# A two-layer graph network on one core: the second layer's tiles in a new order, half of x1 kept on chip

## What is computed

```python
h = jnp.maximum(_layernorm(x), 0.0)
x = x + elu(graph_attention(h, adj) @ W_out + b_out)      # 16 heads, masked softmax
h = jnp.maximum(_layernorm(x), 0.0)
# second layer: q, k, v = h @ W.T + b
z = scale * (q @ k.T) * adj
z = jnp.where(z == 0.0, -10000.0, z)
out = x + relu(softmax(z, axis=1) @ v)
```

## Time and profile before

| | us |
|---|---|
| median of 3 runs | 469.98 (469.42 to 470.12) |
| the profiled execution | 469.46 |
| its span, first to last instruction | 467.5 |
| busy in the span: TensorE, VectorE | 395.3, 369.1 |
| busy: GpSimd, ScalarE | 257.9, 246.1 |

### The profile page before, as it was taken

How to read it: one execution, slowest core, us unless ns; L and a number is a source line. 1 busy time by engine, 2 the same in 40 slices (tenths; PEclk the granted TensorE clock), 3 DMA queues, 4 the chain that set the end, 5 groups by cost and what they waited for, 6 DMA issues and landing times.

```text
span 467.5 us, 6241 instructions
## 1 busy us (share of the span) xinstructions
PE 395.3 (85%) x2058; PEld 282.6 (60%) x2070; DVE 369.1 (79%) x731; ACT 246.1 (53%) x511; POOL 257.9 (55%) x268
## 2 busy tenths in 40 slices
PE   7999999997899998989959879789891998866960
PEld 3888887784777887865737546456581565423430
DVE  4999999987899999977999996898445789957300
ACT  4389777766899998924424433444432433312310
POOL 2335241242788677766757648835337787871330
PEclk9599999999899999999989998899996899995995
DMA  8989998510000123445535527632136678873451
GB/s 315 399 320 332 390 339 299 201 70 2 6 6 5 23 72 92 104 126 182 188 87 166 162 91 205 197 122 91 46 113 192 199 174 168 165 162 43 52 65 19
DMA packets 26997, 70.02 MB, mean 150 GB/s; under 512 B 7893, under 2 KB 8149, under 8 KB 24789
## 3 DMA queue, kind: packets, MB, share of 16 engines
q0 software_dynamic: 13056, 38.45, 31.5%
q1 hardware_dynamic: 13904, 31.16, 18.3%
q10 hardware_dynamic: 4, 0.00, 0.0%
HBM read 52.47 MB, written 17.13 MB: 149 GB/s over the span
## 4 chain that ended last, share of the span: by engine, by line
POOL 31%; PE 15%; issue 15%; DVE 9%; DMA 1%; ACT 1%; DVEq 0%; POOLq 0%
PE psum L1303 8%; POOL s_shared L1231 7%; PE psum L1401 5%; POOL s_shared L1254 4%; POOL out_dram L1243 4%; POOL s_x L1254 4%; POOL s_shared L1212 3%; POOL s_rs L1242 3%; POOL out_dram L1259 3%; DVE s_shared L796 2%; DVE s_shared L794 2%; POOL s_x L1249 2%; DVE s_x L810 1%; DMA w_out<-h_dram,s_near_rank 1%; POOL w_out L1254 1%
## 5 line engine op out<-in xcount | busy, mean ns | idle before, releaser
L1064 ACT ACTIVATE s_shared<-psum,seq_all 128x320 bf16<-128x320 f32 x192 | 81.7, 568 | 6.1 <-PE psum L1303 4.4
L1303 PE MATMUL psum<-s_shared 128*128 128x198 bf16 x768 | 75.2, 254 | 9.6 <-POOL s_shared L1212 9.6
L1303 PEld LDWEIGHTS psum<-s_shared 128*128 128x128 bf16 x768 | 67.9, 98 | 17.4 <-POOL s_shared L1212 9.9
L555 PE MATMUL psum<-w_seq,hT 128*128 128x272 f32 x256 | 63.8, 405 | 0.4 <-ACT w_seq L416 0.4
L1325 PE MATMUL psum<-w_out,hT 128*128 128x512 f32 x128 | 60.7, 619 | 0.4
L555 PEld LDWEIGHTS psum<-w_seq,hT 128*128 128x128 f32 x256 | 49.4, 197 | 10.3 <-ACT w_seq L416 0.5
L1347 PE MATMUL psum<-w_qk,s_early 128*128 128x257 f32 x240 | 54.5, 379 | 0.0
L1347 PEld LDWEIGHTS psum<-w_qk,s_early 128*128 128x128 f32 x240 | 44.4, 190 | 6.0
L1231 POOL DMA_INDIRECT s_shared<-seq_dram,tab x30 | 37.7, 1255 | 11.3 <-issue 8.9
L1325 PEld LDWEIGHTS psum<-w_out,hT 128*128 128x128 f32 x128 | 26.0, 203 | 25.8 <-issue 24.9
L1212 POOL TENSOR_TENSOR s_shared<-s_shared 128x1056 f32<-128x1056 f32 x16 | 31.1, 1945 | 15.2 <-DVE s_shared L796 15.2
(11 more groups left out here) (264 smaller groups left out, 756.8 us busy)
## 6 DMA issues: line engine op xcount, KB each, us to landing
adj_ring<-in_adj_dram SPq DMA_DIRECT2D x16, 1024.0 KB, 8.1
seq_dram<-seq_all POOLq DMA_DIRECT2D x16, 264.0 KB, 4.7
x_ring<-in_x_dram SPq DMA_DIRECT2D x16, 256.0 KB, 8.4
h_dram<-h_t SPq DMA_DIRECT2D x16, 256.0 KB, 2.4
w_seq<-in_L_gnn_W_seq_dram SPq DMA_DIRECT2D x1, 1024.0 KB, 5.7
w_q<-in_L_gnn_W_q_dram SPq DMA_DIRECT2D x1, 1024.0 KB, 13.7
w_k<-in_L_gnn_W_k_dram SPq DMA_DIRECT2D x1, 1024.0 KB, 15.9
w_v<-in_L_gnn_W_v_dram SPq DMA_DIRECT2D x1, 1024.0 KB, 9.0
```

The source lines that it names most:

```text
L555: last = pe.matmul(bank[2 + 2 * (t % 2) + i][:, 0:SX // 2], hT[:, t % 2, c * P:(c + 1) * P], w_seq[:, c, i * (SX // 2):(i + 1) * (SX // 2) ...
L1064: last = act.activation(ind[i][:, j, PAD:], bank[4 + i][:, 0:LN], ACT.Sign, bias=seq_all[:, j, D + n:D + n + 1])
L1303: last = pe.matmul(acc(i)[:, k, 0:3 * W2], ind[i][:, j, k * P:(k + 1) * P], rhs.rearrange("p t w -> p (t w)"), start=(j == 0 and k != 1), ...
```

## The change

In the second layer the tiles come in the order `SEQ1`: the tile without slots first, then rising numbers of slots. The gathers of all 40 slots come ahead of all outputs. They go to other places (`row`): the last ones over the first ones again, and no longer into x1. So tiles of x1 can stay on chip: the first layer scatters only the first eight (`STORED`), for which ScalarE's relu and an accumulating output are kept; for the other eight VectorE adds x1 to the relu of the product (`add_x`) and a plain scatter writes the sum. VectorE's order is written out by hand. TensorE transposes the last h1 tile ahead of query 12, does queries 12 to 14 behind the column sums and 15 behind the transposes of the first tile; the products of the first tile still come ahead of the second tile's transposes. Some of the first layer's gathers are issued one step earlier.

```diff
-GATHER = {0: ((5, 5, 8),), 1: ((7, 0, 3),), 2: ((7, 3, 5),), 3: ((9, 0, 3),), 4: ((9, 3, 4), (11, 0, 2)),
-          5: ((11, 2, 3), (12, 0, 2)), 6: ((14, 0, 2),), 7: ((13, 0, 3),), 8: ((15, 0, 3),)}
+GATHER = {0: ((5, 6, 8), (7, 0, 2)), 1: ((7, 2, 5),), 2: ((9, 0, 3),), 3: ((9, 3, 4), (11, 0, 2)), 4: ((11, 2, 3),),
+          5: ((12, 0, 2),), 6: ((14, 0, 2),), 7: ((13, 0, 3),), 8: ((15, 0, 3),)}
...
-U1_AT = {4: 14, 6: 15}
...
+SEQ1 = [4, 0, 1, 2, 3, 6, 8, 10, 12, 14, 11, 13, 15, 9, 7, 5]
+POS1 = {t: p for p, t in enumerate(SEQ1)}
+ROW1 = {t: sum(SLOTS[i] for i in SEQ1[:p]) for p, t in enumerate(SEQ1)}
+EXP1_AT = {2: 1, 4: 2, 8: 3, 11: 4}
+BASES_AT = {0: (1, 2, 3), 1: (4,), 3: (5, 6, 7), 5: (8, 9), 9: (10, 11, 12), 10: (13,), 12: (14, 15)}
+WEIGHTS_AT = {0: 1, 3: 2, 5: 3, 9: 4, 12: 5}
+STORED = 8
+BY_ACT = [p for p in range(T) if TURN[SEQ1[p]] < STORED]
+BY_DVE = [p for p in range(T) if TURN[SEQ1[p]] >= STORED]
...
         def u_bank(t):
-            return 6 if t >= EARLY or U_NO[t] % 2 else 4
+            return 6 if U_NO[t] % 2 else 4
...
-        o_t = [lone[:, 0, :], lone[:, 1, :], lone[:, 2, :], bv_bc[:, :]]
-        PARTS = [(0, 4), (5, 2), (7, 2), (9, 3), (12, 4)]
-        first_of = {t0: g for g, (t0, n) in enumerate(PARTS)}
-        with_slots = [sum(n > 0 for n in SLOTS[:k]) for k in range(T + 1)]
+        PARTS = [slice(0, 4), slice(6, 11, 2), slice(12, T, 2), slice(9, T, 2), slice(5, 8, 2)]
+        PART_TILES = [len(range(T)[part]) for part in PARTS]
+        FIRSTS = (1,)
+        with_slots = [sum(SLOTS[t] > 0 for t in SEQ1[:p]) for p in range(T + 1)]
...
-        def row(k):
+        ROWS_EARLY = FLAT_ROWS + C + LONE + 1
+        ROWS_AGAIN = ROWS_EARLY + EARLY - 4
+
+        def row(t, s):
+            k = ROW1[t] + s
+            if k >= ROWS_AGAIN:
+                k -= ROWS_AGAIN
             if k < FLAT_ROWS:
                 return shared[:, k * D:(k + 1) * D]
-            if k < FLAT_ROWS + T:
-                return x1[:, k - FLAT_ROWS, :]
-            return w_out[:, k - FLAT_ROWS - T, :]
+            if k < FLAT_ROWS + C:
+                return w_out[:, k - FLAT_ROWS, :]
+            if k < FLAT_ROWS + C + LONE:
+                return lone[:, k - FLAT_ROWS - C, :]
+            if k < ROWS_EARLY:
+                return bv_bc[:, :]
+            return early[:, 4 + k - ROWS_EARLY, 0:D]
...
                 def scores1(g):
...
-                    for t in range(t0, t0 + n):
-                        dot(t)
-                    if t0 == EARLY:
-                        constants(EARLY, T)
...
                 def aggregate1(t):
-                    h = hb[t % 4]
-                    dve.wait_ge(base_ready, t + 1)
+                    p = POS1[t]
+                    h = hb[p % 4]
+                    dve.wait_ge(base_ready, p + 1)
...
+                def add_x(p):
+                    own_x = x1[:, TURN[SEQ1[p]], :]
+                    dve.wait_ge(o_done, p + 1)
+                    dve.scalar_tensor_tensor(own_x, bank[2 + p % 4], 0.0, own_x, ALU.max, ALU.add).then_inc(o_added, 1)
+
+                constants(0, EARLY)
                 dve.wait_ge(h_sum_mm, 1)
                 dve.tensor_copy(h_sum, bank[0]).then_inc(sums_ready, 1)
-                constants(0, EARLY)
+                for t in range(4):
+                    dot(t)
                 scores1(0)
+                dot(6)
                 normalise1(0)
                 for t in range(4):
                     aggregate1(t)
-                for g in range(1, len(PARTS)):
-                    t0, n = PARTS[g]
-                    if g > 1:
-                        for t in range(PARTS[g - 1][0], t0 - 1):
-                            aggregate1(t)
-                    scores1(g)
-                    if g > 1:
-                        aggregate1(t0 - 1)
-                    normalise1(g)
-                for t in range(*(PARTS[-1][0], T)):
-                    aggregate1(t)
+                dot(8)
+                dot(10)
+                scores1(1)
+                add_x(0)
+                constants(EARLY, T)
+                dot(12)
+                normalise1(1)
+                aggregate1(6)
+                dot(14)
+                scores1(2)
+                aggregate1(8)
+                normalise1(2)
+                aggregate1(10)
+                dot(11)
+                dot(13)
+                aggregate1(12)
+                dot(15)
+                dot(9)
+                add_x(4)
+                aggregate1(14)
+                scores1(3)
+                dot(7)
+                normalise1(3)
+                aggregate1(11)
+                dot(5)
+                aggregate1(13)
+                scores1(4)
+                add_x(8)
+                aggregate1(15)
+                normalise1(4)
+                aggregate1(9)
+                add_x(9)
+                aggregate1(7)
+                add_x(10)
+                aggregate1(5)
+                add_x(11)
+                add_x(12)
+                add_x(13)
...
                 copy_u(11)
+                copy_h1T(T - 1)
                 copy_u(12)
-                copy_h1T(T - 1)
...
-                def output(t):
...
-                        act.wait_ge(out_stored[t % 4], 16 * (t // 4))
-                    act.activation(o_t[t % 4], bank[2 + t % 4], ACT.Relu).then_inc(o_ready, 1)
+                def output(p):
+                    act.wait_ge(o_done, p + 1)
+                    act.wait_ge(x1_stored, STORED * 16)
+                    act.activation(x1[:, TURN[SEQ1[p]], :], bank[2 + p % 4], ACT.Relu).then_inc(o_relu, 1)
...
-                    act.wait_ge(weights_ready, g + 1)
...
-                act.wait_ge(none_set, 1)
                 for i in range(2):
                     act.wait_ge(h1_stored[i], T // 2 * 16)
+                base_of(0)
+                copy_u(14)
+                act.wait_ge(none_set, 1)
                 exp_scores1(0)
-                base_of(0)
-                base_of(1)
                 for k in range(T):
                     act.wait_ge(a_tr, k + 1)
                     if k >= 2:
                         act.wait_ge(o_done, k - 1)
                     act.activation(aT[k % 2], bank[k % 2], ACT.Copy).then_inc(aT_done, 1)
-                    if k + 2 < T:
-                        if k + 2 in first_of:
-                            exp_scores1(first_of[k + 2])
-                        base_of(k + 2)
-                    if k >= 1:
-                        output(k - 1)
-                    if k in U1_AT:
-                        copy_u(U1_AT[k])
-                output(T - 1)
+                    if k in EXP1_AT:
+                        exp_scores1(EXP1_AT[k])
+                    if k in WEIGHTS_AT:
+                        act.wait_ge(weights_ready, WEIGHTS_AT[k])
+                    for p in BASES_AT.get(k, ()):
+                        base_of(p)
+                    if k == 0:
+                        copy_u(15)
+                    if k - 2 in BY_ACT:
+                        output(k - 2)
+                for p in (T - 2, T - 1):
+                    if p in BY_ACT:
+                        output(p)
...
-                gather(5, 0, 5)
+                gather(5, 0, 6)
...
-                    pool.indirect_dma_start(out[:, :], bass.IndirectOffsetOnAxis(own[:, SEQ[t], :], 0), x1[:, t, :], None).then_inc(x1_stored, 16)
+                    if t < STORED:
+                        pool.indirect_dma_start(out[:, :], bass.IndirectOffsetOnAxis(own[:, SEQ[t], :], 0), x1[:, t, :], None).then_inc(x1_stored, 16)
...
                 def gather1(t):
                     for s in range(SLOTS[t]):
-                        pool.indirect_dma_start(row(FIRST_SLOT[t] + s), None, h1_dram[:, :],
+                        k = ROW1[t] + s
+                        if k == ROWS_EARLY:
+                            pool.wait_ge(u_done, U_NO[EARLY - 1] + 1)
+                        if k == ROWS_AGAIN:
+                            pool.wait_ge(agg_ready, 4)
+                        pool.indirect_dma_start(row(t, s), None, h1_dram[:, :],
...
-                def put(t):
-                    pool.wait_ge(o_ready, t + 1)
-                    pool.indirect_dma_start(out[:, :], bass.IndirectOffsetOnAxis(own[:, t, :], 0),
-                                            o_t[t % 4], None, compute_op=ALU.add).then_inc(out_stored[t % 4], 16)
...
-                pool.wait_ge(x1_stored, T * 16)
                 pool.wait_ge(proj_done, T)
+                pool.wait_ge(x1_stored, STORED * 16)
                 for i in range(2):
                     pool.wait_ge(h1_stored[i], T // 2 * 16)
-                for t in range(9):
+                for t in SEQ1:
                     gather1(t)
-                for t in range(T):
-                    put(t)
-                    if 9 + t < T:
-                        gather1(9 + t)
-                for i in range(4):
-                    pool.wait_ge(out_stored[i], T // 4 * 16)
+                for p in range(T):
```

(72 more changed lines are left out.)

33 lines of the change are left out of this document (16 added, 17 removed).

## The result

The changed kernel takes 455.85 us (454.85 to 457.15, four runs) against 469.70 of the kernel before in the same comparison: a ratio of 0.971, 95% interval 0.967 to 0.975. The prediction said 456.9.

What follows compares the result with a forecast made beforehand. VectorE was to set the pace from 365.9: 63.8 us of work, 1.5 stall, 9.0 to the last output's issue at 440.2, then 14.2, span 454.4; as median 456.9 us, range 454.0 to 462.0.

Steps and rivals of the forecast that it cites:

- Last h and first gather: End of first layer: fewer stores of x1 make the last h 0.7 us earlier, at 343.4; first gather at 346.8.
- Rival 4: First layer's gather order costs: GpSimd's late power at tile 1 is not covered, +1.0 us, 457.9; chance 0.08.
- VectorE's wait for the base: Start of second layer: VectorE stands from about 363 until the fifth tile's base comes at 365.9, 2.8 us.
- VectorE's work: Second layer, from 365.9 to the end of the last aggregate: dots, aggregates, score blocks, adds and constants sum to 63.8 us.
- The gathers' step: GpSimd's second-layer gathers: 1.35 us each for the first 14 steps, 1.38 for the last 25.
- stall of 1.5 at tile 5's dots: VectorE reaches tile 5's dots at 402.8, the last gather lands at 404.3: 1.5 us lost, bounds 0 and 11.8.
- rival 1: Best case: gathers at 1.32 us a step or less, VectorE never waits for tile 5, 455.4 us; chance 0.22.
- The prediction's own sign: Profile after: last gather issued near 400, right if the mean gather step is 1.34 to 1.41 us.
- rival 3: Second-layer gathers held by busy VectorE: a step of 2.00 us gives 472.4; chance 0.07, of which 0.05 slower than before.
- The end: Behind VectorE's last aggregate: transposes, two products, relu and hand-over to the last output's issue, 9.0 us, from 431.2 to 440.2.
- The clock term: Last tiles' products on TensorE: slowed if a gap lowers the granted clock; counted as 0, bound 1.5 us.
- rival 2: TensorE's clock or small waits at the end: +1.5, +0.8, +0.7 us; 458.4 at one, 459.9 with all; chance 0.18.

## Why the prediction was right, step by step, and where it is not

On the chips of the first runs each term can be set beside its place, all in the profiled execution (span 454.4 predicted, 455.4 measured):

- **Last h and first gather.** TensorE's wait in the first layer went from 1.50 to 0.85 and VectorE's wait of 0.73 is gone. Less the 1.07 of a late start, the last h1 is 0.83 earlier; 0.7 was predicted. The gather order in tile 1 costs nothing: VectorE waits 0.94 there for GpSimd, where it waited 0.93 for rows. Rival 4 is out.
- **VectorE's wait for the base** was 3.85, not 2.8. It stood from 362.97, as predicted, and went on at 366.83 instead of 365.9. This 0.93 is the late start less the first layer's small surplus: counted from the first layer's start the base came when predicted, and VectorE stood longer because it got there 1.1 earlier.
- **VectorE's work** to the last aggregate: 430.20 - 366.83 = 63.4, predicted 63.8. An `add_x` behind an aggregate takes 0.61, the lower bound.
- **The gathers' step** was 1.307 instead of 1.35 and 1.38. The term *stall of 1.5 at tile 5's dots* was mis-sized: it is 0. That is rival 1's mechanism. The prediction's own sign, a mean step of 1.34 to 1.41, didn't come. A little of this stood in the rows of before: the six outputs between the last gathers took 12.1 us, not 6 x 1.94 = 11.6, so a gather there took 1.42 and not 1.44. Of the 40 gathers the groups' means lie between 0.96 and 1.13 us beside a nearly solid VectorE, so rival 3's mechanism doesn't show. (That rival's 25 x 0.52 is 13.0, not 13.1; nothing hangs on it.) By the Trainium skill, page SBUF — State Buffer, section Who interferes with whom, VectorE's two-input instructions would hold the gathers back if a gather's instruction counts as one that reads SBUF; this trace doesn't agree with that reading, at 1.307 a step.
- **The end** from the last aggregate to the last output's issue: 10.62, predicted 9.0. The 1.6 is the slow product (5.29 for 3.65, at a granted clock of 0.66). The clock term counted at 0 with a bound of 1.5 was mis-sized: it came in full, and 0.1 more. That is rival 2's mechanism. It and rival 1's mechanism cancel, which is luck.
- **Behind the last issue** 14.6 us instead of 14.2.

The sum: +0.9 (base), -0.4 (work), -1.5 (stall), +1.6 (product), +0.4 (end) is +1.0 on the span. The profiled execution took 457.15 against 456.4 predicted, the median 455.85 against 456.9: the median was to lie 0.5 above the profiled one and lies 1.3 below it, which is scatter between runs. So the mechanism and the large terms are right, and the closeness within 1 us is in part luck.

The theory that the reorder's parts need each other was tested by leaving each out: without the gathers first 9.9 us are lost, without the prologue 6.7, and the gathers first alone make the kernel before 5.3 slower. The first two are more than the 14 together, so the parts don't add up.

On chip 13 the prediction is wrong: 487.9 lies outside its range and on the other side of no change. The step that failed there is "VectorE waits for this base until 365.9": the base came at 398.3, as ScalarE took up finished work of TensorE 32 us late. Rival 3 had the gathers held by VectorE; what happens is that TensorE's results, recorded as finished, wait while gathers run, and the gathers keep their pace (1.3 a step up to 392.97). No rival had that. Shown are: the stand without any edit, on one chip and in six profiles; its absence in the first profile and on chip 7, where two versions issue the same 40 gathers without a break (the one with all x1 stored and the one with the old prologue); and that in five of the six the second tile's copy comes 4.7 to 6.8 us behind a run of gathers. That the gathers cause the delay isn't shown.

Open are three things. Whether shorter runs of gathers avoid it was to be told by the outputs between the gathers, which didn't meet that chip. Why the kernel before takes 6 us more there isn't known either; its profile on that chip is missing. And whether TensorE finishes late or its signal is late, the records can't say: they model the ends of matmuls. In these traces "remote" stands as the releaser and the gathers show no landing times, so some semaphore events weren't recorded. A part of the recording itself in the delay isn't excluded.

## What to carry to other kernels

Before you move transfers ahead of everything in a queue, see which buffers then come free later: alone the move lost 5 us to one that did. Once an engine sets the pace, price what you add to it, down to 0.6 us steps, against what the addition saves elsewhere; here GpSimd was relieved and VectorE paid. And measure a reordering like this one on more than one chip before trusting its sign.

## What the runs showed that I had not expected

- The same changed kernel is at 0.971 of the kernel before on the chip of the first comparison and at 1.024 on chip 13. The kernel before itself differs much less (469.2 to 470.0 elsewhere, 476 on chip 13).
- On chip 13, ScalarE acted on TensorE's recorded work up to 32 us late in the changed kernel, while 25 gathers were issued between 361 and 393, and up to 40 us late in another version.
- A gap of 2.47 us on TensorE was followed by a product of 5.29 at a granted clock of 0.66, a gap of 1.16 by one of 3.60 at 1.00. So the 1.5 us by which VectorE's last aggregate came earlier brought 1.7 more behind it.
